# Group 2's two choices added by DVE, the tile table and the routing's deviation one chunk sooner, attention weights loaded later, and three more reorderings in a vision tower kernel

## The reference

```python
h = _L0_tok_ref(x, W, b, cls_token, pos_enc)          # patches @ W.T + b, class token, + pos_enc
h = h + _L0_attn_ref(_layernorm(h), ...)              # relative bias, causal softmax
h = h + _L0_ffn_ref(_layernorm(h), ...)               # shared expert + 2 of 7 routed experts, width 704
h = h + _L1_attn_ref(_layernorm(h), ...)
h = h + _L1_ffn_ref(_layernorm(h), ...)               # int weights * 1/127, width 768
# _L0_ffn_ref:
logits = x @ wr.T + rb; probs = softmax(logits); scores, idx = top_k(probs, 2)
scores = scores / scores.sum(axis=-1, keepdims=True)
out = shared_out + sum over e of w[..., e:e+1] * _expert(x, rg[e], ru[e], rd[e])
```

## Time and profile before

| | us |
|---|---|
| median of 3 runs (lowest, highest) | 1035.79 (1035.03, 1036.11) |
| the profiled execution | 1035.61 |
| its span, first to last instruction | 1033.8 |
| PE busy | 959.3 (93%) |
| DVE busy | 712.3 (69%) |
| ACT busy | 660.4 (64%) |
| POOL busy | 360.6 (35%) |

### The profile page before, as it was taken

One profiled execution on the slowest core, in us unless ns is written; L12 is line 12 of the kernel. 1 busy time (PEld: TensorE's weight loads), 2 busy tenths in 40 slices (PEclk: granted clock), 3 DMA queues, 4 the chain that ended last, 5 costly groups with the idle time before them and its releaser, 6 DMA issues.

```text
span 1033.8 us, 29009 instructions
## 1 busy us (share of the span) xinstructions
PE 959.3 (93%) x10725; PEld 883.5 (85%) x10726; DVE 712.3 (69%) x1402; ACT 660.4 (64%) x1206; POOL 360.6 (35%) x285
## 2 busy tenths in 40 slices
PE   4979999979999987999999999999799999799998
PEld 4967888868898987999999999998678888689998
DVE  3536677765656666999999999995467776645443
ACT  3336677865465635777787777776476678565652
POOL 0254354375666740111111211121555545521210
PEclk9999999999999999999999999999899999999999
DMA  6620000008311134111111111212411100000000
GB/s 233 235 106 3 3 3 3 3 3 333 75 37 34 41 77 182 37 36 41 36 36 52 43 41 36 59 46 74 142 26 29 24 3 3 2 13 14 23 24 24
DMA packets 30979, 57.69 MB, mean 56 GB/s; under 512 B 13202, under 2 KB 22418, under 8 KB 29724
## 3 DMA queue, kind: packets, MB, share of 16 engines
q1 hardware_dynamic: 15984, 39.42, 11.8%
q0 software_dynamic: 13664, 15.25, 5.1%
q10 hardware_dynamic: 1228, 1.57, 0.5%
HBM read 41.43 MB, written 14.67 MB: 54 GB/s over the span
## 4 chain that ended last, share of the span: by engine, by line
PE 73%; ACT 10%; DVE 8%; issue 5%; DMA 2%; POOL 1%; DVEq 0%; SPq 0%; ACTq 0%
PE ps L1484 19%; PE ps L1489 16%; PE ps L1491 15%; PE ps L1490 15%; PE ps L1890 3%; PE ps L1641 2%; PE ps L1630 2%; DVE Hd L1196 2%; DMA x_in<-in_xT_dram 2%; ACT L858 1%; ACT Hf_hi L852 1%; ACT Sg L858 1%; PE ps L1778 1%; DVE hsum L1186 1%; ACT RTs L739 1%
## 5 line engine op out<-in xcount | busy, mean ns | idle before, releaser
L1379 DVE TENSOR_TENSOR tile_w<-arena,tile_w 128x704 fp32r<-128x704 f32 x129 | 142.7, 1134 | 23.9 <-ACT tile_w L926 21.4
L584 POOL DMA_INDIRECT routed_out<-yt,tile_to x43 | 42.0, 977 | 262.2 <-DVE yt L1397 261.9
L926 ACT ACTIVATE tile_w<-arena 128x704 fp32r x129 | 122.3, 984 | 0.6 <-issue 0.5
L1489 PE MATMUL ps<-tile_w,xTs 128*128 128x352 f32 x344 | 115.4, 335 | 6.0 <-DVE h L1351 3.3
L1491 PE MATMUL ps<-tile_w,xTs 128*128 128x352 f32 x344 | 112.0, 325 | 0.0
L1490 PE MATMUL ps<-tile_w,xTs 128*128 128x352 f32 x344 | 111.6, 324 | 0.0
L453 POOL TENSOR_TENSOR Km<-KT,cst 128x592 f32<-128x592 f32 x64 | 75.7, 1184 | 77.2 <-PE ps L1484 45.8
L852 ACT ACTIVATE Hf_hi<-Hd 128x296 fp32r<-128x296 f32 x96 | 43.4, 452 | 79.6 <-DVE Hd L1196 78.3
L1196 DVE TENSOR_TENSOR Hd<-Sg,ps 128x296 f32<-128x296 f32 x96 | 44.3, 462 | 69.4 <-ACT Sg L858 68.1
L1075 DVE SCALAR_TENSOR_TENSOR ps<-ps,bias 128x592 f32<-128x592 f32 x64 | 50.1, 783 | 59.0 <-PE ps L1484 59.0
L1489 PE MATMUL ps<-xf_hi,gu_lo 128*128 128x296 f32 x272 | 86.0, 316 | 2.6 <-DVE Hd L1196 2.2
(11 more groups left out here) (232 smaller groups left out, 3081.1 us busy)
## 6 DMA issues: line engine op xcount, KB each, us to landing
arena<-in_ew_dram SPq DMA_DIRECT2D x5, 2176.0 KB, 13.4
x_in<-in_xT_dram SPq DMA_DIRECT2D x7, 888.0 KB, 5.8
xt<-routed_in SPq DMA_DIRECT2D x43, 129.0 KB, 2.0
arena<-in_ew_dram POOLq DMA_DIRECT2D x2, 2176.0 KB, 11.3
yg<-routed_out SPq DMA_DIRECT2D x6, 512.0 KB
out_dram<-h SPq DMA_DIRECT2D x8, 296.0 KB, 2.7
routed_in<-zero_x SPq DMA_DIRECT2D x12, 129.0 KB, 5.4
gu_i<-in_gu_dram SPq DMA_DIRECT2D x1, 1536.0 KB, 10.3
```

The lines of the kernel that those rows point to most:

```text
L926: act.activation(tile_w[half][0][:, cols], gate_up_of(w, half)[:, cols], ACT.Copy).then_inc(s.wh, 1)
L1379: dve.tensor_tensor(tile_w[half][1][:, cols], gate_up_of(w, half)[:, cols], tile_w[half][0][:, cols].bitcast(F32), ALU.subtract).then_inc( ...
L1489: pe.matmul(out_, w[1], x[0], start=start, stop=False)
```

## The change

Six edits:

1. ACT issues the loads of `qkv_w` and `out_w` after the upper part of group 1's patches, in place of second and third of all. PE's wait for these loads moves from the start of attention 0 to the first logits.
2. In the routing of FFN 0 the copy of the first rows moves from `at` 2 to 1, the deviation (table load, logarithm, exponential), `r_exp`, DVE's `norm` and PE's second transposes and variance from 3 to 2, the second copy from 4 to 3. The squares stay at 2, the slots and counts at 4.
3. The table of tiles begins behind the last chunk of group 5, and its pieces in group 6 come after chunks 1, 2 and 3 in place of 0, 2, 3 and 4.
4. PE's wait for FFN 0's last addition moves behind tile 0's gate and up products.
5. Around the start of attention 1: the squares of group 0 go ahead of the last down weights' copy (ACT), the normalised group 0 ahead of the last tile's result (DVE), the weights' upper part ahead of `xa_hi` (ACT), the centring and the weights' lower part ahead of `xa_lo` (DVE). The addition of group 2's choices goes from POOL to DVE, in front of the first scores' scaling.
6. The last group's output is stored in two halves, each after its own addition.

```diff
-            with sp.Fori(0, GROUPS) as g:
+            with sp.Fori(0, GROUPS - 1) as g:
...
+            for m in range(DK):
+                sp.wait_ge(F[1].y, FREE + 2 * GROUPS - DK + m + 1)
+                sp.dma_start(out[:, m, group(GROUPS - 1)], h[:, m, group(GROUPS - 1)]).then_inc(s_out, 16)
@@ pool, attention
-                if l == 1:
-                    sum_routed(2, 0, 1)
@@ scalar
             act.dma_start(cst[:], consts).then_inc(s_cst, 16)
-            act.dma_start(qkv_w, qkv0).then_inc(s_attw, 16)
-            act.dma_start(out_w, wo0).then_inc(s_attw, 16)
...
             upper_patches(1, 1, 16)
+            act.dma_start(qkv_w, qkv0).then_inc(s_attw, 16)
+            act.dma_start(out_w, wo0).then_inc(s_attw, 16)
@@ scalar, attention
                 if l == 1:
                     act.wait_ge(E.y_mm, TILES)
+                act.activation(qkv_p[0], (qkv_w, qkv_w1)[l], ACT.Copy).then_inc(s_upper, 1)
+                if l == 1:
                     upper_x(a, 0, 0, xa[0])
-                act.activation(qkv_p[0], (qkv_w, qkv_w1)[l], ACT.Copy).then_inc(s_upper, 1)
@@ scalar, ffn
-                    if at == 2:
+                    if at == 1:
                         sent_before(act, r)
                         rows(r, r % 2, 0, 7)
+                    if at == 2:
                         if r + 1 < GROUPS:
                             squares(s, r + 1)
-                    if at == 3:
                         act.preload_act_table_set("natural_log_exp_and_others")
                         if r + 1 < GROUPS:
                             deviation(s, r + 1, 6)
                         r_exp(r)
-                    if at == 4:
+                    if at == 3:
                         rows(r, r % 2, 1, 7)
@@ scalar, routed
+                squares(A[1], 0)
                 upper_down(TILES - 1)
-                squares(A[1], 0)
@@ vector, attention
-                else:
-                    dve.wait_ge(a.xh, 1)
-                    dve.tensor_tensor(xa[0][1], xn[0][:], xa[0][0].bitcast(F32), ALU.subtract).then_inc(a.xl, 1)
                 dve.wait_ge(a.xn, FREE + 1)
                 centre(a, 1, 6)
                 if l == 1:
...
+                    dve.wait_ge(a.xh, 1)
+                    dve.tensor_tensor(xa[0][1], xn[0][:], xa[0][0].bitcast(F32), ALU.subtract).then_inc(a.xl, 1)
+                    dve.wait_ge(s_gat[0], 64)
+                    dve.tensor_tensor(yg[0][:, :, 0], yg[0][:, :, 0], yg[0][:, :, 1], ALU.add).then_inc(C.sum, 1)
                 scaled(0, 0)
@@ vector, ffn
-                    if at == 3 and r + 1 < GROUPS:
+                    if at == 2 and r + 1 < GROUPS:
                         norm(r + 1)
...
+                        if l == 0 and g == GROUPS - 3 and j == 5:
+                            next(pieces)
@@ vector, routed
-                tile_out(TILES - 1, 0)
...
                 dve.tensor_tensor(xn[0][:], cen[:], rsd[:].unsqueeze(1).to_broadcast([P, DK, N]),
                                   ALU.mult).then_inc(A[1].xn, 1)
+                tile_out(TILES - 1, 0)
@@ tensor
+                        pe.wait_ge(s_attw, 16 * 7)
                         logits(0, 0, 0)
...
-                        if at == 3:
+                        if at == 2:
                             pe.wait_ge(s.rowA, FREE + r + 1)
                             token_rows(r, r % 2, 1, 7)
...
                 gate_up_half(0, 0, 0)
                 gate_up_half(0, 0, 1)
                 tile_in(1, 1, 0)
+                pe.wait_ge(F[0].y, FREE + 2 * GROUPS)
                 over_tiles(pe, step)
...
             pe.wait_ge(s_cst, 16)
-            pe.wait_ge(s_attw, 16 * 7)
...
-            pe.wait_ge(F[0].y, FREE + 2 * GROUPS)
...
-TABLE_AT = 1, 0, 1, 1, 2, 0
+TABLE_AT = 0, 1, 1, 2, 0, 0
```

More of the change, by code:

```diff
@@ L437, in _ @@
                     load_routed(2 * i + b, b, yg[b])
-            with sp.Fori(0, GROUPS) as g:
+            with sp.Fori(0, GROUPS - 1) as g:
                 sp.wait_ge(F[1].y, FREE + 2 * g + 2)
                 sp.dma_start(out[:, :, group(g)], h[:, :, group(g)]).then_inc(s_out, 16)
-            sp.wait_ge(s_out, 16 * GROUPS)
+            for m in range(DK):
+                sp.wait_ge(F[1].y, FREE + 2 * GROUPS - DK + m + 1)
+                sp.dma_start(out[:, m, group(GROUPS - 1)], h[:, m, group(GROUPS - 1)]).then_inc(s_out, 16)
+            sp.wait_ge(s_out, 16 * (GROUPS + 1))
         @block.gpsimd
```

## The result

| | before | changed kernel |
|---|---|---|
| median of the runs beside each other | 1036.08 us (6 runs) | 1029.13 us (6 runs) |
| ratio to before | | 0.9925, 95% interval 0.9908 to 0.9943 |
| span of the profiled execution | 1033.8 us | 1027.4 us |
| mean granted clock in it | 0.981 | 0.985 |

The change gains 7.0 us in the median and 6.4 in the span; 16.1 were forecast, and the time lies above the range. The question is where nine microseconds went. I take starts of the same instruction in both traces and subtract: the lead of the changed kernel (in us; negative when the changed kernel is behind).

The account below looks back on a forecast made before the run. PE was taken as the bound, with 73% of the chain, so removing its idle waits pays. Terms 2.0 + 0 + 4.6 + 2.7 + 6.7 + 0.1 = 16.1 us gave 1019.6 us, range 1013 to 1026.

Parts of the forecast that it names:

- edit 4's: Tile 0 not held by FFN 0's last addition: tile 1 starts at about 405.0 instead of 408.08; 2.7 us, bounds 1.2 and 3.2.
- the clock term of edit 5: Attention 1, after the removed wait for POOL's sum: matmuls partly at 0.50 clock; full speed gives back up to 2.5 us.
- edit 3's clock: FFN 0's tile table: the clock drop following the removed 1.9 us wait goes too, 1.5 of the 4.6 us.
- edit 2's balance: FFN 0's seven routings: each loses 1.2 to 2.5 us, gains its logits wait; net 0, bounds -4 to +4.
- edit 1's load: Opening: group 2's patches load starts near 11.7 instead of 14.06, not held up by the moved weights; 2.0 us taken.
- rival (d): FFN 0: new variance wait costs seven routings 1.9 us plus a clock drop each, 23 us in all, 1043; chance 0.04.
- (d)'s milder case: FFN 0 routings: a smaller cost of the new variance wait, time 1026 to 1036; chance 0.06.
- Rival (c): Attention 1: gather shares DMA with 2.3 MB of weights, lands about 731, DVE's sum wins nothing; 1026.3; chance 0.15.
- The hold of the sum by POOL's norm operation: Attention 1 prologue: POOL's norm operation may block DVE's sum for 1.5 us, making edit 5 worth 5.2.
- Edit 6, 0.1 forecast: Last output: half starts one addition sooner, 0.42 us, but the last half sets the end; 0.1, bounds -0.2 and 0.4.

Follow-up runs that it names:

- Rows only: Changed kernel with only half of edit 2: second transposes and both row copies a chunk sooner, variance, exponentials and DVE's norm in their old chunk; 1025.05 us, ratio 0.9909.
- bare sum: Kernel before with only the addition of group 2's choices moved from POOL to DVE, none of edit 5's reorderings; 1032.8 us, ratio 0.9963.
- variance only: Changed kernel with only edit 2's variance, logarithm, exponentials and DVE's norm a chunk sooner, transposes and row copies in old chunks; 1040.1 us, ratio 1.0045.

## Why the prediction was wrong, point by point

No single term carries the miss. In the traces the steps that failed are edit 4's (2.2 us short: it left out the wait for tile 2's rows), the clock term of edit 5 (4.0 of the 6.7 us were kept), edit 3's clock (2.0 short in the first trace, 0.6 in most), edit 2's balance (1.4) and edit 1's load (1.0).

- **Edit 1, 2.0 forecast, 1.0 measured.** ACT's start gained 1.84, as said. The load of group 2's patches started at 12.39 instead of 14.06 (forecast 11.7), and took 8.11 us instead of 7.60. In the thirteen traces with edit 1 it takes 7.85 to 8.28 us, in the five without 7.35 to 7.88. The two weights issued at 11.57 and 11.96 are in its company; that they are the reason is argued, not tested. The Trainium skill ("DMA: Bandwidth & Descriptors", "Why a DMA increments its semaphore by 16 and not by 1") made it 2.4, because the late engine carries only a sixteenth of them; the trace shows less than half of that. The start (1.67 us sooner, not 2.4) accounts for 0.7 of what is missing, the longer load for 0.5.
- **Edit 2, 0 forecast: this step failed.** The new wait was seen and nearly right in size (1.2 to 1.9 forecast, 0.9 to 1.5 measured), and rival (d)'s drops of the clock behind it did not come. The time lies in (d)'s milder case, 1026 to 1036, but for the most part not by its mechanism. Wrong was the other side of the balance: I set against it the logits' waits as if they were slack to be won. Rows only shows that they aren't. My forecast of 17.8 us for a routing was good, but I compared it with single periods between 17.1 and 19.5 and left out the last, of 15.4: seven routings took 122.5 us before, 17.5 each, so it meant 2.1 lost, and 1.4 to 1.5 were. Undoing the edit gains about 5 us in medians, of which I can place the 1.5 and, in some executions, the late drop.
- **Edit 3, 4.6 forecast; 4.0 measured** in nine traces, 2.1 to 3.0 in four, 2.6 in the first, whose clock stood at 0.58 from 362 to 366 us. The step was right; the clock term is what varies: the nine lose nothing to slow clock there, the four 0.9 to 1.7 us.
- **Edit 4, 2.7 forecast, 0.5 measured.** The step up to tile 1 was right: 2.9 us with edit 2 undone, alone and in the changed kernel's second trace, 1.8 in its first, whose tile 0 ran at half speed. It stopped one tile too early, and the result lies below its bound of 1.2. I asked what is late next for PE among engines, and not what SP's load of tile 2's rows meets: 4.4 MB issued 9 to 10 us before and still in flight. The trace of the kernel before had it: the rows landed 0.3 us after the weights and 0.65 before PE came. The chain's blame on the experts' weights, which I put aside, pointed at the right load.
- **Edit 5, 6.7 forecast, 6.6 measured at scores 3, 4.0 kept.** Gather 6.0 us (6.2 forecast), sum 1.74 (1.2), ACT's wait for the weights 3.60 (2 to 3). Rival (c) did not come. The hold of the sum by POOL's norm operation, priced at 1.5 us, came with 0.5: the operation runs from 722.60 to 724.05, the sum from 723.38. Where DVE's sum began first, in the bare sum, it took 1.22 us and POOL's operation 1.95 instead of 1.44. What failed is "full speed would give back up to 2.5": the slow stretch moved behind 748 us, out of the cover of ACT's wait, and took 2.6 back.
- **Edit 6, 0.1 forecast, 0.8 measured.** The last transfer has half the bytes and its twin is already under way: from the start of the last pair of additions to the end 3.22 us instead of 4.05.
- **Range.** Its upper end, 1026, meant a gain of 9.6 us; 7.0 came. It had no room for several small terms at once: five of six came out below their middle, by 1.0 to 2.7 us each.

## What to carry to other kernels

Ask of each wait that an edit removes which engine would be the next late one, and test it before counting the wait as gain: here moving work in front of its input cost more (10.3 us of waits) than the waits it was to remove (5.0). Follow a sooner start down to the next small transfer, and look at which large one is in flight and when it lands: the slack there (0.65 us here) is the most that the sooner start can gain. Time that stands beside an engine's wait for something else, a slow clock too, is worth nothing when it goes, and costs where it comes again uncovered.

## What the runs showed of the hardware

- **Behind the same wait the clock drops in one execution and not in another.** Behind PE's 2.73 us wait at 54 to 56 us the clock fell in twelve of the eighteen traces (1.7 us lost each time) and stayed up in six. The two traces of edit 2 undone, the same kernel, differ in where attention 1's drop comes. In the kernel before the sum of all such losses varies from 14.4 to 23.9 us between executions, which is most of their spread of 10 us. In the seven routings of FFN 0 it fell behind one of seven waits of 0.9 to 1.5 us in the first trace of the changed kernel and behind none in the second, and behind five of seven of 2.2 to 2.7 us with the variance only.
- **A small load behind a large one** (129 KB of rows, 4.4 MB of weights from another engine's queue) landed 0.17 to 0.34 us after it in fifteen traces. That made 4.8 to 5.9 us when issued 8 to 9 us behind the second large load and 10.2 when issued 4 behind it, against 2.0 to 2.1 alone.
- **POOL and DVE block each other, and which one pays is chance of phase.** In the changed kernel's first trace POOL's early sum started 0.02 us ahead of DVE's long subtraction: POOL took its 2.39 us, DVE 3.85 instead of 1.61, and PE waited 1.13 us. In its second trace POOL started 0.11 us behind the same subtraction: POOL took 3.77, DVE 1.62. In the kernel before POOL took 3.68 and DVE lost less. The Trainium skill ("SBUF — State Buffer", "Who interferes with whom") says this of two-input DVE operations and GpSimd; the trace agrees, and it explains the 0.6 us lost among the tiles, where nothing was edited; the second trace loses nothing there. Timelines of DVE and POOL:

```profile
569.00 3.85 DVE L1384 TENSOR_TENSOR tile_w<-arena,tile_w 128x1408 fp32r<-128x1408 f32 x1
...
568.98 2.39 POOL L591 TENSOR_TENSOR yg_early<-yg_early 74x1024 f32<-74x1024 f32 x1 [3.25 <-DMA routed_out<-yt,tile_to]
```
